# Metaformer layer on one core: attention in blocks of five rows, the second group's taps spread among the first group's images, and the normalised sum recomputed in the last stage

## The reference, cut to what matters

```python
# x: (4, 256, 48, 48), float32
def attn_kernel(x):                        # 49 weights per pixel
    k = relu(conv(x, w1, 7x7, dilation 2, padding 6) + b1)   # 256 -> 128 channels
    k = relu(batch_norm(conv1x1(k, w2) + b2))                # 128 -> 49
    return softmax(k, axis=1)
def conv_ref(x):                           # every pixel: weighted sum of its 49 dilated neighbours
    return sum over p of shift(x, 2 * (p // 7), 2 * (p % 7)) * attn[:, p]
x = x + conv_ref(ln_c(x))                  # ln_c, ln_t: (v - mean) / sqrt(var + eps) over the channels
t = tokens(x)                              # (4, 2304, 256)
n = ln_t(t)
# ffn_ref(n): softmax router on the mean of n over the tokens of a batch, top 2 of 8 experts,
#   y = sum of weight_e * (gelu(n @ W1[e] + b1[e]) @ W2[e] + b2[e])
#   return layer_norm(y + n) * gamma + beta
t = t + ffn_ref(n)
```

## Time and profile before

| | |
|---|---|
| median of 3 runs | 1289.99 us (1288.7 to 1295.73) |
| the profiled execution's own time | 1290.51 us |
| its span | 1288.6 us |
| busy: PE, DVE, ACT, POOL | 88%, 56%, 39%, 18% of the span |
| mean granted TensorE clock | 0.898 |
| convolution up to its first product | 0 to 143.6 us |
| convolution | to 555.75 us |
| attention | to 812.0 us |
| experts | to 1289 us |

### The profile page before, as it was taken

How to read it: one execution, slowest core, us unless ns; L and a number is a source line. 1 busy time by engine, 2 the same in 40 slices (tenths; PEclk the granted TensorE clock), 3 DMA queues, 4 the chain that set the end, 5 groups by cost and what they waited for, 6 DMA issues and landing times. The chain is left out here.

```text
span 1288.6 us, 19335 instructions
## 1 busy us (share of the span) xinstructions
PE 1128.8 (88%) x7380; PEld 980.9 (76%) x7380; DVE 715.9 (56%) x1719; ACT 496.7 (39%) x923; POOL 237.4 (18%) x160
## 2 busy tenths in 40 slices
PE   3766899999999999939877978689899989989997
PEld 2665667667666666639877968589899989989997
DVE  3445345356355243414673664456777776776776
ACT  4444333232332201114353354364454455455442
POOL 1000000000000000010251353203322331332332
PEclk9969899999999999755885687689999999999999
DMA  9210021112102000060894297404214211421211
GB/s 272 82 37 19 19 74 38 38 39 87 37 1 73 17 1 16 1 134 3 220 264 113 58 269 204 150 25 148 74 50 133 77 51 60 147 73 37 75 50 37
DMA packets 98968, 106.34 MB, mean 83 GB/s; under 512 B 5298, under 2 KB 95699, under 8 KB 98692
## 3 DMA queue, kind: packets, MB, share of 16 engines
q1 hardware_dynamic: 79888, 86.15, 23.4%
q10 hardware_dynamic: 19000, 19.11, 4.8%
HBM read 65.69 MB, written 39.56 MB: 82 GB/s over the span
## 5 line engine op out<-in xcount | busy, mean ns | idle before, releaser
L729 PE MATMUL pM<-V,U 128*128 128x368 f16 (+3 forms) x2016 | 319.3, 315 | 0.0
L729 PEld LDWEIGHTS pM<-V,U 128*128 128x128 f16 x2016 | 196.7, 98 | 107.2 <-issue 0.8
L1507 DVE TENSOR_TENSOR gl<-gf,gh 128x384 fp32r<-128x384 f32 x192 | 161.9, 864 | 63.6 <-ACT gh L1401 63.6
L1401 ACT ACTIVATE gf<-pH,b1c 128x384 f32<-128x384 f32 x192 | 112.0, 583 | 193.3 <-PE pH L1620 143.2
L1635 PE MATMUL pY<-w2h,gh 128*128 128x256 f32 x576 | 167.4, 291 | 17.4 <-DVE z L1519 16.4
L1635 PE MATMUL pY<-w2l,gh 128*128 128x256 f32 x576 | 163.1, 283 | 0.0
L1635 PE MATMUL pY<-w2h,gl 128*128 128x256 f32 x576 | 162.9, 283 | 0.0
L521 DVE TENSOR_TENSOR V<-pV,V 128x384 f16<-128x384 f32 x96 | 53.1, 556 | 179.7 <-ACT V L407 179.4
L1620 PE MATMUL pH<-xh,w1h 128*128 128x384 f32 x384 | 131.5, 343 | 9.3 <-DVE xl L1500 4.6
L407 ACT CAST V<-pV 128x384 f16<-128x384 f32 x96 | 45.6, 477 | 225.8 <-PE pV L700 225.7
L1620 PE MATMUL pH<-xl,w1h 128*128 128x384 f32 x384 | 130.7, 340 | 0.0
(11 more groups left out here) (173 smaller groups left out, 1539.2 us busy)
## 6 DMA issues: line engine op xcount, KB each, us to landing
xa<-in_xt SPq DMA_DIRECT2D x16, 576.0 KB, 5.0
xn_scratch<-xa SPq DMA_DIRECT2D x16, 576.0 KB, 6.0
xn<-xn_scratch SPq DMA_DIRECT2D x16, 576.0 KB, 8.6
xr<-in_xt SPq DMA_DIRECT2D x16, 576.0 KB, 6.3
t_scratch<-ts ACTq DMA_DIRECT2D x16, 576.0 KB, 5.3
tn_scratch<-tn ACTq DMA_DIRECT2D x16, 576.0 KB, 5.3
tnk<-tn_scratch SPq DMA_DIRECT2D x24, 384.0 KB, 3.3
tk<-t_scratch SPq DMA_DIRECT2D x24, 384.0 KB, 3.9
```

What stands on the lines that cost most here:

```text
L729: return nc.tensor.matmul(out[:, :, first:end], U[:, hi_u, k, piece, :], V[:, b % 2, hi_v, k, c, :, first + TILES * d:end + TILES * d], st ...
L1401: last = nc.scalar.activation(dst, pH[:, j % 4, 0:CN], ACT.Gelu, bias=b1c[:, j // FB, j % FB:j % FB + 1])
L1507: tt(gl[:, sl, j, :], gf[:, j % 2, :], gh[:, sl, j, :].bitcast(F32), ALU.subtract).then_inc(g_step, 1)
```

## The change

**Convolution.** The hand-written lists at the start give way to one loop in which a turn of U and a turn of V alternate: `for pair: for j: turn_u(j); turn_v(j) of image pair + 1`, with `ln` of image pair + 2 on DVE after j = 0, `magnitude` on ACT after j = 1 and 3, `normalise_x` after j = 2, and `tap_scale` and `bound` of the next pair after j = 5. The batch norm's small operations are all done after the first pair. `bound` writes another bank (`pM[:, 2]`).

**Attention.** Blocks have 5 rows (120 partitions), so an image has 5 blocks, the last with 96 rows. An image takes 39 matmuls of 256 columns instead of 48. A group's spreading has 44 items of 6 matmuls, with 80 columns (64 in 8 of the items) that lie 120 elements apart, against a table of 120 columns, on three banks instead of four. A has a buffer for each group, and the second group's 44 items are issued in 21 portions behind the three sums of images 1 to 7 (`mixed`); ACT then copies two of three, DVE the third. tn stays on the core: it is summed for the router and no longer stored. ts is stored as soon as it is summed. Loads and stores are in two parts (four blocks, and the last). The orders on DVE and ACT change as the diff shows, and the token sums are taken once a batch.

**Experts.** tn is no longer loaded. It is recomputed from t for each chunk three ahead: `statistics` on DVE between `take_x` and `sum_up`, `scale_x` on POOL, three activations (`normalise`) on ACT behind `take_x`. t has three buffers.

```diff
+            for pair in range(PAIRS_OG):          # PE; ACT and DVE have the same loop
+                for j in range(U_PAIR):
+                    turn_u(U_PAIR * pair + j)
+                    if j < V_TURNS and pair + 1 < BI:
+                        turn_v(V_TURNS * (pair + 1) + j)
+                    if j == SCALE_AT and pair + 1 < PAIRS_OG:
+                        bound(pair + 1)
...
+BROWS = 5
+TB = BROWS * SIDE
+NB = -(-SIDE // BROWS)
-SLOT = 4
-SBANKS = OBANKS = 4
+SLOT = 6
+SBANKS, OBANKS = 3, 4
-        A = sb("A", [TT, BLK, 2 * BT, TT], F16)
+        A = sb("A", [TB, GROUPS, BLK, 2, GI, NB, TB], F16)
...
+            for n in range(IMGS):                 # ACT, attention
+                for u in range(T_SUMS):
+                    for item in mixed(n, u):
+                        if item % DVE_SHARE < DVE_SHARE - 1:
+                            spread_out(act, nc.scalar.copy, NU + item, a_by_act)
+                    if u == 0 and n > 0:
+                        store(n - 1)
+                        normalise(n - 1)
+                if n + 2 < IMGS:
                     x_high(n + 2)
-                if n > 0:
-                    normalise(n - 1)
-                    store(n - 1)
...
             for n in range(IMGS):                 # DVE, attention
                 sums(n)
-                if (n + 1) % GI > 0:
-                    statistics(n)
-                    if n + 2 < IMGS:
-                        x_low(n + 2)
+                if n + 2 < IMGS:
+                    x_low(n + 2)
+                statistics(n)
...
                     last.then_inc(o_ready, 1)     # PE, attention, after the sums of image n, part u
+                    for item in mixed(n, u):
+                        spread_taps(NU + item)
...
+            def scale_x(b, m):                    # POOL, experts
+                n, s = CHUNKS * b + m, m % 2
+                pool.wait_ge(x_step, (n + 1) * X_STEPS)
+                if not (is_first(b) and m < 2):
+                    pool.wait_ge(tn_made, 2 * (n - 1))
+                nc.gpsimd.tensor_tensor(xrs[:, s], xve[:, s], mhalf[:, :], ALU.pow).then_inc(x_scaled, 1)
+                pool.wait_ge(x_scaled, 2 * n + 1)
+                nc.gpsimd.tensor_tensor(xsh[:, s], xnm[:, s], xrs[:, s], ALU.mult).then_inc(x_scaled, 1)
+            def normalise(b, m):                  # ACT, experts
+                n, s = CHUNKS * b + m, m % 2
+                act.wait_ge(x_scaled, 2 * (n + 1))
...
+                for t in range(CT):
+                    last = nc.scalar.activation(tnk[:, s, t, :], tk[:, m % TBUFS, t, :], ACT.Identity,
+                                                bias=xsh[:, s, t:t + 1], scale=xrs[:, s, t:t + 1])
+                last.then_inc(tn_made, 2)
+            def statistics(b, m):                 # DVE, experts
...
+                dve.wait_ge(tk_loaded[m % TBUFS], 16 * (CHUNKS // TBUFS * b + m // TBUFS + 1))
+                for t in range(CT):
+                    s.did(nc.vector.bn_stats(xst[:, t, :], tk[:, m % TBUFS, t, :]))
+                for t in range(CT):
+                    s.did(nc.vector.bn_aggr(xmv[:, t, :], xst[:, t, :]))
+                s.did(nc.vector.tensor_scalar(xve[:, sl], xmv[:, :, 1], 1e-5, None, ALU.add))
+                s.did(nc.vector.tensor_scalar(xnm[:, sl], xmv[:, :, 0], -1.0, None, ALU.mult))
...
                     if later(b, m, 2, CHUNKS):
                         take_x(*later(b, m, 2, CHUNKS))
+                    if later(b, m, 3, CHUNKS):
+                        statistics(*later(b, m, 3, CHUNKS))
                     if m == CHUNKS - 2 and later(b, m, 2, CHUNKS):
                         split_w1(b + 1)
                     sum_up(b, m)
```

More of the change, by code:

```diff
@@ L619, in a_low @@
                        ALU.subtract).then_inc(alo_ready, 1)
[L621 to L627, removed]
             ln(0)
             ln(1)
[L631 to L635, removed]
@@ L648, in _ @@
[L648 to L657, removed]
+            for j in range(V_TURNS):
+                v_low(j)
+            tap_scale(0)
@@ new lines, in _ @@
+            for pair in range(PAIRS_OG):
+                for j in range(U_PAIR):
+                    u_low(U_PAIR * pair + j)
+                    if j < V_TURNS and pair + 1 < BI:
+                        v_low(V_TURNS * (pair + 1) + j)
+                    if j == LN_AT and pair + 2 <= BI:
+                        ln(pair + 2)
+                    if j == SCALE_AT and pair + 1 < PAIRS_OG:
+                        tap_scale(pair + 1)
+                if pair == 0:
+                    dve.wait_ge(par_loaded, 16 * 7)
+                    s = Steps(dve, bn_step, 0, BN_STEPS)
+                    s.did(nc.vector.tensor_scalar(bnp[:, 5:6], bnp[:, 4:5], 1e-5, None, ALU.add))
+                    s.did(tt(bnp[:, 0:1], bnp[:, 0:1], bnp[:, 3:4], ALU.subtract))
+                    dve.wait_ge(bn_rstd, 1)
+                    s.did(tt(bnp[:, 7:8], bnp[:, 6:7], bnp[:, 1:2], ALU.mult))
+                    s.settle()
+                    s.did(nc.vector.tensor_scalar(w2s[:, :], w2s[:, :], bnp[:, 7:8], None, ALU.mult))
+                    s.did(stt(bnp[:, 0:1], bnp[:, 0:1], bnp[:, 7:8], bnp[:, 2:3], ALU.mult, ALU.add))
+                    s.at(BN_STEPS)
@@ L1038, in _ @@
-            for n in range(IMGS):
-                if n % GI == 0:
-                    spread_out(act, nc.scalar.copy, n // GI, 0, a_by_act, x_high)
-                    x_high(n + 1)
-                if (n + 1) % GI > 0 and n + 2 < IMGS:
+                else:
+                    act.wait_ge(pads_set, 4 + n)
+                for t in range(NB):
+                    rows = rows_of(t)
+                    last = nc.scalar.activation(tn[0:rows, n % 2, t, :], ts_[0:rows, n % 2, t, :], ACT.Identity,
+                                                bias=shift[0:rows, n % 2, t:t + 1],
+                                                scale=rstd[0:rows, n % 2, t:t + 1])
@@ new lines, in sum_tokens @@
+            def sum_tokens(b):
+                pe.wait_ge(acc_step, (BI - 1) * (b + 1))
+                for c in range(CC):
+                    at = c * B + b
+                    for t in range(NB):
+                        last = nc.tensor.matmul(pC[:, at:at + 1], acc[:, b % 2, t, c * P:(c + 1) * P], ones[:, :],
+                                                start=(t == 0), stop=(t == NB - 1))
+                last.then_inc(sums_ready, 1)
+            for item in range(NU):
+                spread_taps(item)
@@ L1174, in _ @@
-            last.then_inc(sums_ready, 1)
+                if n > BI and n % BI == 2:
+                    sum_tokens(n // BI - 1)
+            sum_tokens(B - 1)
 EXPERTS, TOPK, FH = 8, 2, 512
@@ L1411, in _ @@
             split_w2(0)
+            normalise(0, 2)
             def body(b):
```

460 lines of the change are left out of this document (237 added, 223 removed).

## The result

The changed kernel takes 1325.78 us (median of 4 runs, 1314.1 to 1327.93) against 1289.35 for the kernel before: 1.0254 times as long, 95% interval 1.0184 to 1.0323. The forecast was 1297 with a range of 1266 to 1322. The profiled execution has a span of 1326.1 us, 37.5 more than the 1288.6 of before.

The account below looks back on a forecast made before the run. It saw PSUM chain latency bounding the start, slow-clocked PE attention, and DVE without slack before PE's awaited addition in experts. -25 - 26 + 56 = +5, plus one for bubbles, gave 1297 us, range 1266 to 1322.

Parts of the forecast that it names:

- 80 cost 0.137: Attention, spreading: a matmul with 80 moving elements takes 0.137 us, so a group takes 34.9 us instead of 39.3.
- 12.5 us of a mixed image: Attention, images 1 to 7: 12.5 us each, taken between 11.6 and PE's 13.5 at 1.2 GHz; -14 us.
- The start: Convolution stage: reordered turns bring the first product at 118 us against 143.6, -25 us (bounds -32 and -15).
- 17 x 1.78 = 30: Experts' stage: statistics of 1.78 us delay the addition PE waits for in 17 ordinary chunks, +30 us.
- the three changes' 18: Experts' stage, transitions: normalise ahead of split_w1 lengthens the chain by 6.1 us, three times, +18 us.
- no slack: Experts' stage: DVE has no slack before adding z of block 0, which PE's third block awaits; the row shows 0.
- the wait of 9 us leaves PE at 1.2 GHz for some microseconds, 1.3 each: 4: Experts' stage, transitions: the clock drop behind three waits of 9 us costs 1.3 us each, +4 us.
- the weights' columns: Attention rival: weight columns pace spreading, 53.9 us a group, total 1340; chance 0.13 shared with the serial reading.
- load and stream in series: Attention rival: weight load and stream add up, 44.2 us a group, total 1316; chance 0.13 shared with weight-paced spreading.
- the ring: Attention: x_high, x_low, statistics, power, normalise wait on each other in a circle, 9.4 us an image; at least 11.6 mixed.
- -25 - 26 + 56: Whole kernel: start -25, attention -26, experts +56 us, summing to +5.
- The statistics hide: Experts' rival: DVE has a gap, so the stage costs +15, total 1254; chance 0.17, wholly or half hidden.

Follow-up runs that it names:

- e3_start_only: The kernel before with the changed kernel's convolution stage alone (one loop of alternating turns); 1258.75 us, ratio 0.9772 to the kernel before.
- e12_before_pool: The kernel before, with POOL's tb addition for the next chunk waiting until DVE has made xl; 1277.25 us, ratio 0.9895 to the kernel before.
- e11_pool: The changed kernel, with POOL's tb addition for the next chunk waiting until DVE has made xl; 1279.07 us, ratio 0.9932 to the kernel before.
- e1_slot: The changed kernel with statistics moved inside sum_up, between additions of blocks 1 and 2, and split_w1 ahead of normalise at expert changes; 1278.0 us.
- e4_forms: The changed kernel with five forms of spreading matmul (element distance, weight columns) in the first group's items, output not the reference's; 1320.76 us, measured once.
- e5_unmixed: The changed kernel with the second group's 44 items issued together behind image 7 instead of spread over images 1 to 7; 1338.52 us.
- e2_ring: The changed kernel with ACT's x_high(n + 2) ahead of normalise(n - 1) again in the attention stage; 1318.09 us.
- e7_compact: The changed kernel with weights aT reordered so a spreading matmul's pixels from an image lie side by side, not 120 elements apart; 1307.32 us.

## Why the prediction was wrong, point by point

The measured time lies above the range, by terms in two stages: attention, whose -26 became -6, and the clock in the experts' stage, 4 us in the sum and about 20 in the trace. The step that failed in attention is the pace of a spreading matmul ("80 cost 0.137"), and with it the 12.5 us of a mixed image.

**The start** was right, in its parts too. The first U turn starts at 28.1 (forecast 28.4); the three pairs and the last then take 25.4, 23.3, 22.3 and 15.2 us (forecast 27, 23.5, 23.5 and 16). First product at 114.35 (forecast 118), -30 for -25, the convolution behind it untouched, and e3_start_only gives the same gain alone.

**Experts: the waits** were right. The waits for z rose by 67.8 - 21.7 = 46 us; "17 x 1.78 = 30" and the three changes' 18 make 48. A wait at such a change is 9 us, as forecast. The reason was incomplete. That DVE has "no slack" in front of that addition was taken as given; e12_before_pool shows that POOL's additions made it so in the kernel before (21 waits became five), and e11_pool that over 1 us of each wait in the changed one was theirs.

**Experts: the clock** was one of the terms that failed. "the wait of 9 us leaves PE at 1.2 GHz for some microseconds, 1.3 each: 4" counted the three long waits alone. The stage lost 72 us: 46 in waits, 6 at its start (forecast 4.3), and 20 beside, of which third blocks at 1.2 GHz are 17.9 - 2.9 = 15, one wait of 3.3 us is one for which the trace shows no cause, and 2 us are unassigned. Waits of 1.7 to 2.1 us in every chunk were enough for the clock to fall in some of them; behind the 0.4 to 1.3 us of e1_slot and e11_pool it fell in none. The four runs of the changed kernel spread over 14 us, and the fastest has the highest mean clock (0.891, the others 0.875 to 0.879), so that this is probably where the spread comes from. Which chunk it takes I did not settle.

**Attention, spreading** was wrong in its size. "80 cost 0.137" is right for elements 96 apart (0.138 in e4_forms), but with five rows they lie 120 apart, and there they cost 0.160. I had taken the number of elements as the whole of the matter: 40.4 instead of 34.9 us for the first group, and 0.023 us more for each of the 264 among the images. Both rivals (the weights' columns; load and stream in series) are wrong as well: 96 columns changed nothing. What was right is that the clock has no part in this pace (2.10 and 2.14 us for twelve at 1.00 and 0.50).

**Attention, mixed images** was wrong by 14 us. "Between 11.6 and 13.5 I take 12.5": PE is the bound, most of the time at 1.2 GHz, and not the ring. At 1.2 GHz throughout, with the spreading at 0.160, it is 39 x 0.213 + 38 x 0.160 = 14.4 us an image. Measured: (111.2 - 6.3 - 4.4 - 1.9) / 7 = 14.1, with image 0, a sum of tokens and two waits taken off. e5_unmixed confirms the bound: without the spreading the same images come at the ring's 9.3 us. The sum's own 13.5 for 1.2 GHz was exceeded because its 5.0 us of spreading were too short. Of the 14 us, 6 are that price, 5 come from taking 12.5 where PE at 1.2 GHz needed more, and the rest a sum of tokens (4.4 for 2.4) and two waits (1.9), less 1 at image 0.

**Attention, the ring** was right (9.26 for 9.4; the last eight images and the end took 85.5 us for 83, though the terms given for the 83 add up to 81.5), and e2_ring shows that it was not worth its whole price, since the loads stand behind it. The stage: forecast -26, measured -6; against the forecast that is +6 in the first group, +14 in the images, +2.5 at the end and -2 at the load of aT.

**The sum.** -25 - 26 + 56 became -30 + 1.5 - 6 + 72. Against the forecast the start gave 5 us more; attention missed by 20 and the experts' stage by 16, both upwards, and that put 1326 above a range that ended at 1322. The statistics' 30 us and the changes' 18 were right, so this is no miss of the main mechanism but of two prices beside it. "The statistics hide" was the rival that I gave 0.17. e11_pool brings the changed kernel part of the way there: 43 of the stage's 72 us are gone, and it is still 29 us longer than before, where that rival had 15.

## What to carry to other kernels

When an engine has no slack ahead of the work that others wait for, look first at whether one of its instructions there takes longer than the same instruction elsewhere in the trace, and at who runs beside it: here two lines on POOL took 43 us off the last stage of one kernel and 8 off that of the other (47 and 13 off the totals). New work in a saturated queue belongs where that queue waits for another engine (between two additions, between two gelus), and its consumers' queues have to be looked through in the same way. A wait of 2 us on PE in each turn of a loop is to be costed with the clock that it may bring down, and a scattered moving operand by the distance of its elements, not by their number alone. Two edits that gain little apart can gain more together, where each uncovers what the other removes.

## What the runs showed of the hardware that I had not expected

- A DVE operation with two inputs in SBUF (gl, 0.56 us) stands still while POOL adds two tiles in SBUF: 3.54 us for two with 4.6 us of POOL additions beside them, 1.88 with 2.5. The slowed pair ends 0.42 us behind the end of POOL's tb in both kernels (865.11 and 864.69; 910.29 and 909.87). POOL pays as well: tb takes 1.84 us in e11_pool and 2.15 beside gl. bn_stats, with one input, is not slowed (0.42 us beside POOL's addition in e11_pool, 0.41 without it in the changed kernel); a tensor_scalar of three elements is (xve, 0.56 for 0.17). The Trainium skill's page SBUF — State Buffer, section Who interferes with whom, has an exclusive lock on a port pair that the two engines share; the traces agree.
- A matmul with 49 rows, 120 columns of weights and 80 moving elements takes 0.160 us with the elements 120 apart, 0.138 with 96 and 0.100 with runs of five side by side, all at a granted clock of 0.50. At 1.00 the first stays at 0.160 and the last falls to 0.058. The Trainium skill's page SBUF — State Buffer, section Door 1: The DMA port swizzle, says that an access that goes to a new 16-byte line pays a penalty. That agrees with the gain from side by side; it does not tell 96 from 120 apart, and the measurement decides.
- With the elements side by side the pace follows the columns of weights, 0.100 us for 120 and 0.082 for 96, at a granted clock of 0.50. The Trainium skill's page TensorE: Matmul & The Clock Gate, section LDWEIGHTS (loading the stationary operand), gives P / 1.2 ns, so 100 and 80: the runs agree at that clock. At 1.00 twelve such matmuls with 120 columns start 0.058 us apart (666.4 us in e7_compact), less than the page's 100 ns, and there the measurement decides.
- The granted clock fell in 11 of 20 third blocks behind waits of 1.7 to 9 us, and not in the other nine behind waits of 1.7 to 2.1 us.
